# Attention products twelve blocks behind their scores, low parts ten and high parts nine, with four loads moved in ScalarE's order

## The reference

```python
x = x + attention(layernorm(x), ctx, ctx, gamma)     # 8 heads of 128 channels per batch, length 1024
    # qk = einsum('bhdq,bhdl->bhql', qh, kh) / sqrt(128);  sm = softmax(qk)
    # ret = einsum('bhql,bhdl->bhdq', sm, vh) * gamma
x = x + mixture(layernorm(x), U, V, W1, b1, W2, b2)  # relu(x W1 + b1), softmax router, 8 low-rank experts
```

## Time and profile before

| what | value |
|---|---|
| median of 3 runs | 1675.27 us (1674.51 to 1677.02) |
| the profiled execution, its own time | 1674.71 us |
| its span in the profile | 1672.9 us |
| PE busy in the span | 1568.3 us (94%) |
| DVE, ACT, POOL busy in the span | 993.9, 765.2, 716.2 us |
| granted TensorE clock, mean over the span | 0.991 |

### The profile page before, as it was taken

The page is one execution under the profiler, slowest core; times in us unless marked ns, Lnnn a source line. Parts: engine busy times, 40 slices in busy tenths (PEclk is TensorE's granted clock), DMA queues, the critical chain, the costliest instruction groups (busy, mean ns, idle before and its releaser), DMA issues.

```text
span 1672.9 us, 21715 instructions
## 1 busy us (share of the span) xinstructions
PE 1568.3 (94%) x6496; PEld 1159.6 (69%) x6496; DVE 993.9 (59%) x1290; ACT 765.2 (46%) x1222; POOL 716.2 (43%) x523
## 2 busy tenths in 40 slices
PE   5999999999999999989868999999999999999999
PEld 3666666666666666666546787877878787787877
DVE  7888888888988888888755432323323232332312
ACT  5676767767777677776653312122121212212120
POOL 3888888878888888887751000000000000000000
PEclk9999999999999999999988999999999999999999
DMA  5899898998989989899785021120302122030302
GB/s 174 265 286 288 262 298 285 279 290 265 298 284 279 289 266 299 278 272 280 249 270 196 0 101 51 70 81 19 132 0 100 50 69 81 15 135 0 101 1 76
DMA packets 119962, 294.18 MB, mean 176 GB/s; under 512 B 26240, under 2 KB 31360, under 8 KB 119936
## 3 DMA queue, kind: packets, MB, share of 16 engines
q1 hardware_dynamic: 97904, 229.87, 42.9%
q10 hardware_dynamic: 22032, 63.97, 12.8%
HBM read 125.87 MB, written 33.69 MB: 95 GB/s over the span
## 4 chain that ended last, share of the span: by engine, by line
PE 52%; POOL 12%; issue 11%; DMA 9%; SPq 6%; DVE 5%; ACT 4%; ACTq 1%; POOLq 0%; DVEq 0%
PE scores L954 21%; PE scores L997 11%; PE attended L1015 11%; POOL pt_lo L331 8%; SPq L223 5%; DMA x_res<-in_x 5%; DMA pt<-pb 3%; PE scores L543 3%; PE spare L1034 2%; DVE pb L606 2%; PE attended L565 2%; DVE neg_max L597 2%; POOL k_lo L314 2%; POOL x_out L340 2%; ACT q L435 1%
## 5 line engine op out<-in xcount | busy, mean ns | idle before, releaser
L331 POOL TENSOR_TENSOR pt_lo<-pt,pt_hi 128x512 fp32r<-128x512 f32 (+1 forms) x256 | 400.4, 1565 | 123.8 <-ACT pt_hi L403 123.4
L427 ACT ACTIVATE probs<-scores,neg_max 128x1024 f32<-128x1024 f32 x256 | 284.6, 1112 | 207.2 <-DVE neg_max L597 206.7
L597 DVE TENSOR_REDUCE neg_max<-scores 128x1 f32<-128x1024 f32 x256 | 312.7, 1221 | 105.6 <-PE scores L543 104.7
L606 DVE STREAM_TRANSPOSE pb<-probs 128x1024 f32<-128x1024 f32 x256 | 316.3, 1236 | 7.8 <-DMA pt<-pb 4.9
L879 POOL TENSOR_TENSOR rstd<-var_eps,minus_half 128x1 f32<-128x1 f32 x28 | 17.2, 614 | 609.7 <-DVE var_eps L1080 609.7
L543 PE MATMUL scores<-k_hi,q_hi 128*128 128x512 f32 x512 | 237.8, 545 | 21.4 <-ACT probs L427 12.1
L565 PE MATMUL attended<-pt_hi,v_hi 128*128 128x512 f32 x320 | 141.0, 440 | 77.1 <-POOL pt_lo L331 76.2
L403 ACT ACTIVATE pt_hi<-pt 128x512 fp32r<-128x512 f32 (+1 forms) x256 | 186.6, 729 | 45.9 <-DMA pt<-pb 45.8
L898 ACT ACTIVATE hidden<-scores,b_col 128x512 f32<-128x512 f32 x64 | 44.2, 690 | 351.4 <-PE scores L954 351.4
L954 PE MATMUL scores<-nt_hi,w_hi 128*128 128x512 f32 x512 | 200.9, 392 | 2.5 <-DVE w_lo L1105 2.5
L954 PE MATMUL scores<-nt_lo,w_hi 128*128 128x512 f32 x512 | 200.3, 391 | 0.0
(11 more groups left out here) (95 smaller groups left out, 2640.4 us busy)
## 6 DMA issues: line engine op xcount, KB each, us to landing
pt<-pb SPq DMA_DIRECT2D x512, 256.0 KB, 4.9
gain_row<-gains SPq DMA_DIRECT2D x64, 256.0 KB, 4.7
x<-x_out SPq DMA_DIRECT2D x64, 256.0 KB, 5.8
first_n<-x SPq DMA_DIRECT2D x32, 512.0 KB, 3.8
result<-x SPq DMA_DIRECT2D x64, 256.0 KB, 3.8
out<-result SPq DMA_DIRECT2D x64, 256.0 KB, 2.0
x_res<-in_x ACTq DMA_DIRECT2D x31, 512.0 KB, 7.0
k_raw<-in_ctx ACTq DMA_DIRECT2D x30, 512.0 KB, 5.4
```

Source lines behind the costliest of these rows:

```text
L331: nc.gpsimd.tensor_tensor(pt_lo[2 * parity + half][:, :, keys, :], pt[2 * parity + half][:, :, keys, :], as_f32(hi[half][q][:]), ALU.subtr ...
L427: nc.scalar.activation(probs[j % 2][:], scores[j % 2][:], ACT.Exp, bias=neg_max[:, j:j + 1], accum_out=row_sum[b][:, j:j + 1]).then_inc(s_ ...
L597: nc.vector.tensor_reduce(neg_max[:, j:j + 1], scores[j % 2][:], AX_X, ALU.max, negate=True).then_inc(s_max, 1)
L606: nc.vector.transpose(pb[half][:, :, j % HALF, :], probs[j % 2][:]).then_inc(s_blocks, 1)
```

## The change

The distances become three constants of their own: products 12 blocks behind the scores, low parts 10, high parts 9. Every engine's slot is rearranged. The first four heads are written out instead of two, since with a distance of 12 the third and the fourth head still refer to heads that don't exist.

- SyncE: the spread of the second half's gains moves from behind the first gather of the same slot to the head of the next slot, ahead of the second gather. The first gather is now issued ahead of the spread of the first half's gains and of the write of the second half's. Its wait on `s_pv` goes.
- GpSimd: `low_queries` from j = 5 to j = 6, `low_keys` from 1 to 2, `low_values` from 3 to 7, the scale from 2 to 3. The two halves' `add_residual` now stand at j = 3 and 5, both for head h - 2. In the tail the residual of the last head comes behind all low parts.
- ScalarE: gains, `high_keys`, q and its high part one block later; `high_values` from j = 2 to 6. The load of the values moves from block 5 to block 1 of the next head, k from 3 to 4, x from 4 to 5, the float32 values from 2 to 5, the residual from 5 to 6.
- VectorE: the scalings of both halves now stand at j = 0 and j = 4 and belong to head h - 2; before they stood at j = 2 (head h - 2) and j = 6 (head h - 1). The inverse sums move there as well, statistics from j = 0 and 1 to 1 and 2, the variance from 2 to 3.

```diff
-    LAG = 10
+    LAG = 12
+    LOW_LAG = 10
+    HIGH_LAG = 9
```

SyncE's slot:

```diff
         def slot(h, n, parity, first, last):
             known = isinstance(h, int)
-            more = not (known and h + 2 >= heads)
+            if not (known and h < 2):
+                spread_gain(h - 2, 1)
             if not first:
                 gather(h - 1, n - JB, 1, 1 - parity)
                 send_gain(h - 1, 0)
...
-            if not (known and h < 2):
-                sp.wait_ge(s_pv, n - JB)
+            gather(h, n, 0, parity)
             if not first:
                 spread_gain(h - 1, 0)
-            if not first:
                 send_gain(h - 1, 1)
             if not (known and h < 2):
                 store_x1(h - 2, 1)
-            gather(h, n, 0, parity)
-            if not first:
-                spread_gain(h - 1, 1)
```

ScalarE's slot, in the loop over j (without the gains):

```diff
                 exps(n + j, j, parity)
...
-                high_probs(quarter_in(h, n, j, parity, LAG - 2))
-                if j == 0 and not last:
+                high_probs(quarter_in(h, n, j, parity, HIGH_LAG))
+                if j == 1 and not last:
                     high_keys(h + 1, n + JB, 1 - parity)
-                if j == 2:
+                if j == 1 and not first:
+                    act.wait_ge(s_vlo, h)
+                    load_v(h)
+                if j == 6:
                     high_values(h, n, parity)
-                    if not first:
-                        load_v_native(h, parity)
-                if j == 3 and more:
+                if j == 4 and more:
                     act.wait_ge(s_klo, h + 2)
                     load_k(h + 2)
-                if j == 4 and more:
+                if j == 5 and more:
                     act.wait_ge(s_q32, h + 2)
                     load_x(h + 2)
...
                 if j == 5 and not first:
+                    if not (known and h < 2):
+                        act.wait_ge(s_pv, n - JB)
+                    load_v_native(h, parity)
+                if j == 6 and not first:
                     if not (known and h < 2):
                         act.wait_ge(s_added, h * 2 - 2)
                     load_residual(h - 1)
-                if j == 3 and not last:
+                if j == 4 and not last:
                     queries(h + 1, 1 - parity)
                     high_queries(h + 1, n + JB, 1 - parity)
```

VectorE's scalings:

```diff
-                if j == 2 and not early:
-                    scale_attended(h - 2, n - 2 * JB, 1)
...
-                if j == 6 and not first:
-                    scale_attended(h - 1, n - JB, 0)
+                if j in (0, 4) and not early:
+                    scale_attended(h - 2, n - 2 * JB, j // 4)
```

More of the change, by code:

```diff
@@ L187, in over_heads @@
         slot(0, 0, 0, True, False)
-        slot(1, JB, 1, False, False)
-        with eng.Fori(1, heads // 2 - 1) as pair:
+        for h in range(1, 4):
+            slot(h, h * JB, h % 2, False, False)
+        with eng.Fori(2, heads // 2 - 1) as pair:
             slot(pair * 2, pair * (2 * JB), 0, False, False)
@@ L353, in slot @@
             for j in range(JB):
-                low_probs(quarter_in(h, n, j, parity, LAG - 1))
-                if j == 1 and not last:
+                low_probs(quarter_in(h, n, j, parity, LOW_LAG))
+                if j == 2 and not last:
                     low_keys(h + 1, 1 - parity)
-                if j == 3:
-                    low_values(h, parity)
[L359 to L366, removed]
+                if j == 3 and not last:
+                    scale_of_queries(h + 1, 1 - parity)
+                if j == 3 and not early:
+                    add_residual(h - 2, 0)
+                if j == 5 and not early:
+                    add_residual(h - 2, 1)
+                if j == 6 and not last:
+                    low_queries(h + 1, 1 - parity)
+                if j == 7:
+                    low_values(h, parity)
                 if last and j in (4, 6):
@@ L379, in gpsimd @@
         for j in range(JB):
[L380 removed]
+            low_probs(quarter_in(h, n, j, 0, LOW_LAG))
+            if j == 1:
+                add_residual(h - 2, 0)
             if j in (1, 2):
                 first_factor(j + 1)
[L383 removed]
+            if j == 5:
                 add_residual(h - 2, 1)
[L385 to L387 removed]
+        for j in range(2):
+            low_probs(quarter_in(h + 1, n + JB, j, 1, LOW_LAG))
+        add_residual(h - 1, 0)
         add_residual(h - 1, 1)
@@ L590, in tensor @@
             turn_first(j)
-        for j in range(2):
+        for j in range(4):
             attended_products(quarter_in(h + 1, n + JB, j, 1, LAG))
@@ L661, in slot @@
                 maxima(n + j, j)
-                if j == 2 and not last:
+                if j == 3 and not last:
                     dve.wait_ge(s_stat, h * 2 + 4)
@@ L667, in slot @@
                     blocks(n + j - 1, j - 1, h)
-                if j < 2 and not last:
-                    statistics(h + 1, 1 - parity, j)
-                if j == 2 and not last:
-                    variance(h + 1, 1 - parity)
-                if j == 2 and not early:
-                    scale_attended(h - 2, n - 2 * JB, 1)
-                if j == 3 and not first:
-                    inverse_sums(h - 1, 1, 1 - parity)
-                if j == 6 and not first:
-                    scale_attended(h - 1, n - JB, 0)
-                if j == 7:
-                    inverse_sums(h, 0, parity)
+                if j in (0, 4) and not early:
+                    scale_attended(h - 2, n - 2 * JB, j // 4)
+                if j in (0, 4) and not first:
+                    inverse_sums(h - 1, j // 4, 1 - parity)
+                if j in (1, 2) and not last:
+                    statistics(h + 1, 1 - parity, j - 1)
+                if j == 3 and not last:
+                    variance(h + 1, 1 - parity)
                 if last and j in (3, 5):
```

29 lines of the change are left out of this document (13 added, 16 removed).

## The result

The changed kernel takes 1705.83 us (median of 4 runs, 1702.34 to 1714.98), the kernel before in the same comparison 1676.14 us: a ratio of 1.018, 95% interval 1.0133 to 1.0227. It is slower by 30 us, where 44 us less were forecast; the range of 1600 to 1668 does not hold it.

The account below looks back on a forecast made before the run. Three loops near 23.8 us, over PE's 23.0, plus 0.4 for the crowded gather and half the overlap excess gave 24.5 us a head: 45 less over 28 heads, +1 at the ends, 1631.5 us, range 1600 to 1668.

Parts of the forecast that it names:

- The distances take PE's waits for low parts: Products two blocks later, high and low parts one: PE's 44.6 us of low-part waits go, at most 3.1 us per head.
- The low part of q: Loop from block 0's scores through VectorE, ScalarE and GpSimd: 23.8 us, so PE waits about 0.8 us at those scores.
- SyncE's queue: Loop of both gathers, four short issues, the gains' write landing and gaps: 23.8 us a head, 22.3 to 25.1.
- the three that were summed: Steady-part loops at about 23.8 us: low part of q, SyncE's queue, and the DMA engines' 0.91 share of 26.1 us.
- The crowded loads: Loads on ScalarE's queue in blocks 4 to 6 beside the first gather: 0.4 us a head, between nothing and 1.8.
- Start and end: Start 0 to -3, last head's read-back tiles +2, tail residual 1 won; both ends together about +1 us.
- The sum: Steady part: 24.5 us per head, bounds 23.0 and 25.6, against 26.1 before; 45 us less over 28 heads.
- The signs of a wrong forecast: Wrong if PE still waits for low parts, or VectorE waits for gathers by more than 1 us a head.
- The round trip of the gains: Rival, chance 0.10: SyncE's loop is 27.3 us with slow gathers and landing; 36 us more, 1711.
- PE becomes the bound: Rival, chance 0.13: quick landing and well-overlapping loops, a head takes 23.3 us; 78 us less, 1597.
- The gather is slowed by the loads: Rival, chance 0.18: SyncE's queue loop gets 1.4 us longer, a head takes 25.3 us; 1655.
- The change only moves the wait: Rival, chance 0.05: PE's waits return at the scores, from exponentials held up by VectorE; within 0.2% of before.

Follow-up runs that it names:

- e4: The kernel before with products 11 blocks behind the scores instead of 10, high and low parts at 8 and 9, all orders kept: 1656.05 us, ratio 0.9893.
- e3: The changed kernel with k loaded in block 3 and the float32 values in block 4 again: 1692.89 us, ratio 1.0121.
- e6: e5 with k loaded in block 3 and the float32 values in block 4, as in e3: 1677.62 us.
- e11: Best kernel: changed kernel with each spread mid-gather, first half's store behind first gather, k loaded in block 3, float32 values in 4: 1618.91 us, ratio 0.9677.
- e2: The changed kernel with the second half's spread behind the second gather instead of ahead of it: 1712.42 us, ratio 1.0236.
- e1: The changed kernel with the first half's spread issued after two of the first gather's eight DMAs: 1689.98 us, ratio 1.0096.
- e5: The changed kernel with the first spread after four of the first gather's eight DMAs and the second behind the second gather: 1645.24 us, ratio 0.9844.
- e7: The changed kernel with VectorE's scaling of the first half at j = 2 instead of 0, SyncE's order kept: 1677.77 us, ratio 1.0019.
- e9: The changed kernel with each spread issued after four of the eight DMAs of its gather: 1642.55 us, ratio 0.9815.

## Why the prediction was wrong

*The distances take PE's waits for low parts* held: 44.6 us went to none in the list, and e4 shows the same effect with nothing moved on SyncE, worth 18 us by its ratio. ScalarE's wait for gathers and GpSimd's for the residual went too, as forecast. None of it shortened a head, since a longer loop had taken over.

*The low part of q* as a loop of 23.8 us: never reached in the changed kernel (PE waits 8.7 us in 22 pieces of 0.5 at most, about 0.4 a head where 0.8 was forecast). The best kernel, at 24.27 a head, comes within half a us of it and still has 9.0 us of that wait; no run tests the sum any closer.

*SyncE's queue* is the step that failed. It was right that the second spread would wait for the write ahead of it: 64.3 us in 22 waits, 2.9 each, where some 4 were forecast. It overlooked that the queue already had such a wait, 62.5 us at the first spread, so that this part of the loop was moved and not added. Without its wait at the store (51.0 us in 22 heads, 2.3 each) SyncE's own round in the changed kernel is 27.25 - 2.3 = 24.9 us, where 23.8 was forecast: a miss of 1.1 us, but not the bound. The bound was a path that the step left out. The change also puts the *first* spread behind all eight DMAs of the first gather, and gives the scaling that reads it only two blocks more, from j = 6 of one slot to j = 0 of the next, where the rest of the head is queued behind it. The reckoning had both moves in the diff and the order (its row of `gain_row_112` behind the gather) and priced the spread as a short issue. Its time was never set against the scaling that reads it. With rows of the kernel before it could have been: four blocks of VectorE and a scaling (2.3 x 4 and 1.0, with the other small work 12.0), the gather at 7.24 to 8.43, a landing of a spread of about 4.7 (median of the kernel before), a few gaps: 24.4 to 25.6. That is a loop longer than each of the three that were summed, but still shorter than the 26.1 us of a head before: finding it would have taken much of the gain out of the forecast, but not turned its sign. The rest is size. The first gathers took 9.3 us to issue in the middle, against 8.2 before and 7.47 in the sum, and their spreads 5.3 us to the scaling. Why the first gathers grew, with no byte more in a head, is open; moving two loads back (e3) left them at 9.2.

*The crowded loads* were priced at 0.4 us a head, bounds 0 and 1.8, as a longer gather. e3 measures 27.25 - 26.83 = 0.42 for moving two of the loads back. That the sizes agree is partly luck, since the gather accounts for only 0.1 of it. And the same edit is worth +32 us in one order of SyncE and -19 in another, so the term had no sign of its own. In e6 the loss is the landing of the spread that closes a loop; in e11 the gain is not explained. The Trainium skill (DMA: Bandwidth & Descriptors, "Queues, rings and completion order") has the engines take turns between queues with work. By that rule a load issued beside a gather lands late, and the landing of the values agrees, 7.4 us in the changed kernel and 7.5 and 4.5 in the pair above; it does not say which of the two hurts, and that was the question.

*Start and end*, +1: 32.6 less 31.7 is 0.9. The sum came out, its parts did not: the start costs 74.70 - 73.51 = 1.2 us, where 0 to -3 was forecast, and the end -0.3, where +2 and -1 were. In the last head VectorE waits for the read-back tiles

```profile
867.25 1.28 DVE L647 BATCH_NORM_STATS2 stats<-first_n 128x6 f32<-128x512 f32 x2 [9.03 <-DMA first_n<-x]
```

2.9 us longer than in the earlier trace rows, near the forecast 2.

*The sum*: 24.5 us a head with bounds of 23.0 and 25.6, against 27.25. The bounds were made from the loops that had been found and from the gathers' times before, and both were too small. The signs of a wrong forecast had the same gap: PE waits for no low part and VectorE for no gather in the changed kernel, so neither sign came, and the forecast was wrong.

*The rivals.* "The round trip of the gains" was priced at 1711, 5 us from the result, and is still not the reason. Taken away alone (e2) it gives nothing, and it had asked for both gathers at 8.43 and a landing of 6.2, where the trace has 8.69 and 7.70 and a landing of 4.1 (median). It is a real cost of the second rank: with the first spread early it is what SyncE waits for (e1), and of the changed kernel's orders in e1, e2, e5 and e7 only the one without either cost (e5) beats the kernel before. "PE becomes the bound" never came: the best kernel's head takes 24.27 us against PE's 23.0. "The gather is slowed by the loads" was right about the gather, 1.1 us longer than before, but e3 does not show the loads to be the reason. "The change only moves the wait" describes best what the profile looks like, though the wait moved to another place than named, and grew.

*Open*: why the loads' places give 19 us in e11; neither expectation had a gain. The landing of the values got shorter, that of k longer (4.5 to 6.3), and SyncE's wait for transposes went from 59.0 to 36.2 us; which of these carries it was not separated.

## What to carry to other kernels

When a change reorders the issues of an in-order queue, follow *every* one that moved to the instruction that reads it, and close each into a loop (reader, what is queued behind it, what the queue then waits for, the issue time of everything ahead, the landing); a bound over only the loops one thought of is too narrow. A small DMA with an early reader belongs neither behind a batch of big ones nor, if it must wait for a landing, in front of one: in the middle of the batch, in e5 and e9, the wait was over or short and the issue time ahead was halved. Where two such waits stand side by side, undo both before judging either.

## What the runs showed of the hardware

Issuing is not free behind other issues. A spread takes 0.35 us on SyncE where it had been waiting, and 0.50 and 1.33 right behind a gather in the rows above; the eight DMAs of a gather take 7.24 to 9.26 us in the rows shown here, about 1 us each. That issue time stood ahead of the first spread.

A write of 2 KB takes as long as a large transfer: the medians from issue to landing of the write of the gains, 4.1 us in the changed kernel and 6.1 in e6, lie beside the 5.1 to 5.3 us of the gathers' DMAs of 256 KB.

The granted clock of PE is 0.98 in the window of the changed kernel and 0.97 in those of e2 and e6, against 1.00 in the earlier trace rows and in e5's. PE's busy time alone doesn't say which: e1 and e7 both have 548.32 of 600 us, at 0.98 and 1.00. No run separates what the clock costs.
